# A Mamba block and a mixture of experts in one program: where a token tile's choice of experts stands, and which steps follow it

## The reference

```
xz = x @ W_in.T;  xs, z = halves of 512 channels
xc = silu(conv_4_taps(xs) + conv_b)            # causal, per channel
dt = xc @ W_x[:32].T
y  = xc * softplus(dt @ W_dt.T + b_dt) * silu(z)
x  = layernorm(2x + y @ W_out.T)

scores = sigmoid(x @ gate_w.T)                 # 16 experts in 4 groups
keep the 2 best groups (by their two best, with a bias), in them the 4 best experts
w = 2.5 * scores of the 4 / their sum
x = layernorm(2x + sum_k w_k * expert_k(x) + shared(x))   # each: (silu(x Wg) * (x Wu)) @ Wd
```

## Time and profile before

| | us |
|---|---|
| median of 3 runs | 664.12 |
| lowest, highest | 659.53, 667.1 |
| the profiled execution, its own time | 662.12 |
| its span in the profile | 660.4 |
| mean granted TensorE clock | 0.941 |
| PE busy | 544.3 (82%) |
| DVE busy | 416.6 (63%) |
| ACT busy | 376.1 (57%) |
| POOL busy | 322.4 (49%) |

### The profile page before, as it was taken

How to read it: one execution, slowest core, us unless ns; L and a number is a source line. 1 busy time by engine, 2 the same in 40 slices (tenths; PEclk the granted TensorE clock), 3 DMA queues, 4 the chain that set the end, 5 groups by cost and what they waited for, 6 DMA issues and landing times.

```text
span 660.4 us, 11746 instructions
## 1 busy us (share of the span) xinstructions
PE 544.3 (82%) x3143; PEld 459.7 (70%) x3143; DVE 416.6 (63%) x1123; ACT 376.1 (57%) x969; POOL 322.4 (49%) x361
## 2 busy tenths in 40 slices
PE   6897999999999999866686788788877778786884
PEld 5584767777676867555586687677877677776773
DVE  5795889888897988674442533333333365665686
ACT  4767677686858582813433544555554455556653
POOL 3502122675757576754654355554445555444510
PEclk9999999999999999997797788888898898899888
DMA  7973021323333223288354476444445676866578
GB/s 197 285 253 137 33 98 64 132 98 129 102 125 106 107 93 106 88 290 294 130 189 145 131 232 197 142 145 144 142 138 158 195 249 205 278 202 219 174 287 281
DMA packets 69094, 110.92 MB, mean 168 GB/s; under 512 B 11204, under 2 KB 52421, under 8 KB 68520
## 3 DMA queue, kind: packets, MB, share of 16 engines
q1 hardware_dynamic: 55800, 74.23, 36.2%
q0 software_dynamic: 12672, 35.67, 14.6%
q10 hardware_dynamic: 560, 0.27, 0.1%
HBM read 61.50 MB, written 49.69 MB: 168 GB/s over the span
## 4 chain that ended last, share of the span: by engine, by line
PE 32%; another core or an unknown queue 22%; ACT 19%; DVE 12%; issue 10%; DMA 2%; ACTq 2%; SPq 0%; POOL 0%; POOLq 0%; DVEq 0%
PE psum L824 4%; PE psum L758 4%; PE psum L760 4%; PE psum L759 4%; PE psum L902 3%; ACT y_out L1362 3%; DVE xc L1512 3%; ACT row L1362 2%; PE psum L1042 1%; ACT y_w L1373 1%; ACT y_pair L1362 1%; ACT y_ids L1371 1%; PE psum L793 1%; PE psum L1016 1%
## 5 line engine op out<-in xcount | busy, mean ns | idle before, releaser
L669 POOL DMA_INDIRECT x_buf<-row,row_id x128 | 127.6, 997 | 71.6 <-issue 45.9
L2122 DVE TENSOR_TENSOR e_act<-g_act,psum 128x512 f32<-128x512 f32 x36 | 24.6, 684 | 122.7 <-ACT g_act L1347 97.5
L1032 PE MATMUL psum<-ew_gu_hi,t_hi 128*128 x286 | 90.8, 318 | 1.8 <-issue 1.8
L661 POOL TENSOR_TENSOR m<-xc,zs 128x512 f32<-128x512 f32 x32 | 41.4, 1315 | 100.5 <-DVE shift L1590 57.4
L1034 PE MATMUL psum<-ew_gu_hi,t_lo 128*128 x286 | 87.3, 305 | 1.6 <-issue 1.6
L1033 PE MATMUL psum<-ew_gu_lo,t_hi 128*128 x286 | 87.3, 305 | 1.2 <-issue 1.2
L1347 ACT ACTIVATE g_act<-psum 128x512 f32<-128x512 f32 x36 | 21.6, 601 | 109.2 <-remote 100.1
L747 POOL DMA_INDIRECT y_buf<-y_out,y_ids x56 | 55.2, 985 | 58.1 <-ACT y_w L1373 22.1
L1512 DVE SCALAR_TENSOR_TENSOR xc<-psum,cw_taps,xc 128x511 f32<-128x511 f32 (+2 forms) x96 | 70.8, 739 | 5.3 <-ACT halo_x L1168 3.9
L1042 PE MATMUL psum<-ident,e_act 128*128 128x128 f32 x143 | 26.3, 312 | 53.0 <-DVE e_act L2122 44.3
L1032 PEld LDWEIGHTS psum<-ew_gu_hi,t_hi 128*128 128x128 f32 x286 | 61.8, 216 | 2.6 <-issue 2.6
(11 more groups left out here) (263 smaller groups left out, 1442.7 us busy)
## 6 DMA issues: line engine op xcount, KB each, us to landing
tiles_in<-x_buf SPq DMA_DIRECT2D x143, 144.0 KB
y_pair<-y_buf SPq DMA_DIRECT2D x20, 512.0 KB
y_in<-y_buf SPq DMA_DIRECT2D x12, 512.0 KB, 7.0
xT<-in_x_T SPq DMA_DIRECT2D x8, 512.0 KB
xtok<-in_x_tok SPq DMA_DIRECT2D x8, 512.0 KB
gu_hi_buf<-w_hi_now SPq DMA_DIRECT2D x8, 512.0 KB, 2.6
x_buf<-pad_row SPq DMA_DIRECT2D x17, 144.0 KB
raw_gu<-in_wg_T SPq DMA_DIRECT2D x16, 128.0 KB, 3.3
```

What stands on the lines that cost most here:

```text
L669: nc.gpsimd.indirect_dma_start(out=x_buf, out_offset=bass.IndirectOffsetOnAxis(ap=row_id[t % ROWS][:, b, k:k + 1], axis=0), in_=row[t % RO ...
L1032: pe.matmul(o, t_hi[par][:, k, r], w_hi, start=k == 0, stop=False)
```

## The change

On VectorE, five of the six steps of the choice leave the places between the root's steps and stand at the tile's end, among the subtractions `x1T_low`, `x_low` and `dt_low`. The steps of `place` for tile t-2 move up, from among the second chunk's convolution taps to among the first chunk's. On TensorE, `ranks` stands ahead of `dt_out`'s second half, the fourth block of `shared_down` moves from a tile's end behind the first half of the next tile's `dt_out`, and in tile 6 `dt_total` goes ahead of `gate`. On POOL, the row sends move up by about one block each, in the tiles and in the order behind them, and the results of the first five quads are sent one quad sooner. VectorE's and ScalarE's orders of tile 7 and of the expert stage are unchanged.

```diff
--- before.py
+++ after.py
@@ -677,7 +677,7 @@
 
             def quads_begun(q):
 
-                return min(q + (5 if q < 5 else 4 if q < NQ // 2 else 3), NQ)
+                return min(q + (4 if q < NQ // 2 else 3), NQ)
 
             pool.wait_ge(s["keep_one"], 2)
             pool.wait_ge(s["keep_ready"], N // seq_len)
@@ -696,38 +696,34 @@
             def tile(t):
                 at_least(pool, "y_done", PAIRS * t + 1)
                 gate_product(t, range(2, KI))
-                if t > 2:
-                    send(t - 3, range(3, SUB))
                 if t > 1:
                     send(t - 2, range(0, 1))
-                if t == NT - 2:
-                    return
+                    send_behind(t - 2, 1, "halo_added", PAIRS * (t + 1) + 1)
                 at_least(pool, "norm_ready", t + 1)
                 gate_product(t + 1, range(0, 2))
                 if t > 1:
-                    send(t - 2, range(1, 2))
+                    send(t - 2, range(2, 3))
+                if t == NT - 2:
+                    return
                 halo(t + 2)
                 if t > 1:
-                    send(t - 2, range(2, 3))
+                    send(t - 2, range(3, SUB))
 
             def last_tile(t):
-                send(t - 3, range(1, 2))
-                at_least(pool, "norm_ready", t)
-                gate_product(t, range(0, KI))
-                send(t - 3, range(2, 3))
-                send_behind(t - 3, 3, "res_done", 2 * (t - 2) + 1)
-                send_behind(t - 2, 0, "y_done", PAIRS * t + 1)
-                send_behind(t - 2, 1, "h_done", KS * (t - 1) + 1)
-                send_behind(t - 2, 2, "ln_in", 2 * (t + 1))
-                send_behind(t - 2, 3, "norm_ready", t + 1)
-                send_behind(t - 1, 0, "x1T_l", KD * (t + 1))
-                send_behind(t - 1, 1, "t_l", 2 * KD)
-                send_behind(t - 1, 2, "e_mul", 1)
-                send_behind(t - 1, 3, "a_l", 1)
-                send_behind(t, 0, "res_done", 2 * (t + 1))
-                send_behind(t, 1, "a_l", 2)
-                send_behind(t, 2, "a_l", 3)
-                send_behind(t, 3, "e_mul", 4)
+                gate_product(t, range(2, KI))
+                send(t - 3, range(3, SUB))
+                send_behind(t - 2, 0, "res_done", 2 * (t - 2) + 1)
+                send_behind(t - 2, 1, "y_done", PAIRS * t + 1)
+                send_behind(t - 2, 2, "h_done", KS * (t - 1) + 1)
+                send_behind(t - 2, 3, "ln_in", 2 * (t + 1))
+                send_behind(t - 1, 0, "norm_ready", t + 1)
+                send_behind(t - 1, 1, "x1T_l", KD * (t + 1))
+                send_behind(t - 1, 2, "t_l", 2 * KD)
+                send_behind(t - 1, 3, "e_mul", 1)
+                send_behind(t, 0, "a_l", 1)
+                send_behind(t, 1, "res_done", 2 * (t + 1))
+                send_behind(t, 2, "a_l", 2)
+                send_behind(t, 3, "a_l", 3)
             first_tile()
             for t in range(1, NT - 1):
                 tile(t)
@@ -936,13 +932,15 @@
             def tile(t):
                 x_proj(t + 1, 0)
                 dt_out(t, range(0, 2))
+                if t > 1:
+                    shared_down(t - 2, range(SUB - 1, SUB))
                 gate_turn(t - 1)
                 x_proj(t + 1, 1)
                 z_proj(t + 1, 0)
+                if t > 1:
+                    ranks(t - 2, t)
                 dt_out(t, range(2, KI))
                 shared_up(t - 1, 0)
-                if t > 1:
-                    ranks(t - 2, t)
                 x_proj(t + 1, 2)
                 out_proj_by_pairs(t)
                 z_proj(t + 1, 1)
@@ -953,12 +951,9 @@
                 shared_down(t - 1, range(0, 2))
                 transposes(t)
                 dt_in(t + 1)
-                if t < NT - 2:
-                    shared_down(t - 1, range(2, SUB))
-                    dt_total(t + 1)
+                shared_down(t - 1, range(2, SUB - 1))
+                dt_total(t + 1)
                 gate(t)
-                if t == NT - 2:
-                    dt_total(t + 1)
 
             def spin(n, bank=SPARE_BANK):
 
@@ -1088,7 +1083,6 @@
                     ranks(NT - 1, NT)
 
             t = NT - 1
-            shared_down(t - 2, range(2, 3))
             dt_out(t, range(0, 2))
             shared_down(t - 2, range(3, SUB))
             gate_turn(t - 1)
@@ -1977,28 +1971,30 @@
                 if not placed:
                     gate_logits(r)
                 softplus_product(t, 0)
-                conv(n, 0)
+                conv_tap(n, 0, 1)
+                if placed:
+                    place_rank(p)
+                conv_tap(n, 0, 2)
+                if placed:
+                    place_rows(p)
+                conv_tap(n, 0, 3)
+                if placed:
+                    place_top(p)
                 if t == TABLE_TILE:
                     first_ends()
                 softplus_sum(t, 1)
+                if placed:
+                    place_ids(p)
                 gate_one(r)
                 softplus_product(t, 1)
                 gate_score(r)
                 conv_tap(n, 1, 1)
-                if placed:
-                    place_rank(p)
                 gate_biased(r)
                 conv_tap(n, 1, 2)
-                if placed:
-                    place_rows(p)
                 group_pairs(r)
                 conv_tap(n, 1, 3)
-                if placed:
-                    place_top(p)
                 group_sums(r)
                 conv_halo(n, 0)
-                if placed:
-                    place_ids(p)
                 group_score(r)
                 if t < 2:
                     weights_low(PIECES_OF[t][0])
@@ -2019,17 +2015,12 @@
                 pick_top(r)
                 for b in range(SUB):
                     norm_mean(t, b)
+                norm_var(t)
+                root_bits(var[:, :], half_bits[:, :], "norm_step")
                 choose_compare(r)
-                norm_var(t)
-                choose_place(r)
-                root_bits(var[:, :], half_bits[:, :], "norm_step")
-                choose_above(r)
                 root_guess(rstd[:, :], half_bits[:, :], "norm_step")
-                choose_order(r)
                 root_z(var[:, :], **root)
-                choose_ties(r)
                 root_h(**root_of)
-                choose_sel(r)
                 root_once(**root_of)
                 root_h(**root_of)
                 root_series(root_z_[:, :], root_h_[:, :], "norm_step")
@@ -2044,14 +2035,19 @@
                 else:
                     for i in PIECES_OF[t]:
                         weights_low(i)
+                choose_place(r)
+                choose_above(r)
                 x1T_low(t)
+                choose_order(r)
                 if t < 2:
                     weights_low(PIECES_OF[t][2])
                 if more:
                     x_low(t + 2)
+                choose_ties(r)
                 if t == TABLE_TILE:
                     first_rows()
                 dt_low(n)
+                choose_sel(r)
                 if t < 2:
                     weights_low(PIECES_OF[t][3])
```

## The result

The changed kernel takes 665.99 us (median of 12 runs, 661.40 to 669.68) beside 664.39 (median of 12) for the kernel before in the same session: a ratio of 1.0102, interval 1.0062 to 1.0141. Those medians are only 0.24% apart, and the two profiled executions 0.65 us (662.77 and 662.12, spans 661.0 and 660.4). So the changed kernel is slower, by 1% in the ratio and by less in the medians, where 659 was forecast: inside the range, on the wrong side.

What follows compares the result with a forecast made beforehand. The prediction took the token tiles as bound by TensorE, with nearly all its idle time in one wait before the third dt product. 3.9 + 0.4 + 0.8 + 0.2 - 0.8 = 4.5 us off 662.12, plus 2.0 for the median: 659; range 650 to 668.

Steps and rivals of the forecast that it cites:

- TensorE's order: Token tiles: moving a shared_down block and ranks fills the wait before the third dt product, between 0 and 5.3 us.
- The term of 0.97 a tile: Steady token tiles: net gain of 0.97 us each from TensorE's new order, after a wait of 0.1 to 0.2 before out_proj.
- Tile 6: End of tile 6: the sooner root releases TensorE's shared_down, which waited 1.96 us, for a gain of 0.2.
- the 3.9: Tiles 3 to 6: 4 x 0.97 = 3.9 us gained by TensorE's new order.
- Tile 6 into 7: Gate of tile 6: its 0.76 wait is filled and dt_low comes sooner, gaining 0.8 us, between 0 and 0.9.
- slower rival: Hand-over: three long send runs each hold ScalarE one block longer, 9.9 us lost, to 674; chance 0.12.
- The picks: VectorE: moving picks to the tile's end nets nil there; the root ends about 0.2 us sooner.
- POOL holds nobody up: 0: Token tiles: POOL's reordered row sends and gate products delay no other engine, cost 0.
- The hand-over and the experts: Hand-over and expert stage: 2.8 us gained by one block fewer, 3.6 charged for longer runs, net loss 0.8.
- the mark of 5.3 us: Stretch 273 to 317: quad 0's g_act over 5.3 us later behind its x1T_lo means the slower rival is under way.
- The one block fewer in the experts' stage: Expert stage: one block of four sends fewer is left there, gain 2.8 us, at most 5.1.
- The terms for the tiles: Token tiles: 3.9 for tiles 3 to 6, 0.4 tile 2, 0.8 tile 6 into 7, 0.2 the sooner root.

Runs made afterwards that it cites:

- e9: e1 with POOL's whole program (sends, gate products, tail conditions, first results) as in the kernel before: 659.00 us, 0.9918 of the kernel before.
- e6: The changed kernel with e1's edit and, in tile 6, POOL's last gate product ahead of block 2's row sends: 658.49 us, 1.0026 of the kernel before.
- e7: The kernel before with only five of VectorE's picks moved to the tile's end, choose_compare standing twice: 656.16 us, 1.0005 of the kernel before.
- e10: e6 with the tail's row-send conditions and the first five quads' results as in the kernel before: 663.86 us, 0.9959 of the kernel before.
- e5: The changed kernel with POOL's second gate product of tiles 2 to 6 held until place_rows is over: 658.27 us, 1.0037 of the kernel before.
- e11: e4's kernel on another chip, where ScalarE is held: 670.13 us, 1.0153 of the kernel before.
- e4: The kernel before with only the changed tail conditions for row sends and first five results, on the 548.8 us chip: 548.77 us, 0.9996 of the kernel before.
- e8: The changed kernel itself, measured again in a second session: 659.86 us, 1.0106 of the kernel before.
- e2: The changed kernel with the old tail conditions for row sends and first five results, on the 548.8 us chip: 554.23 us, 1.0096 of the kernel before.
- e3: The changed kernel with the edits of e1 and e2 together, on the 548.8 us chip: 549.27 us, 1.0003 of the kernel before.
- e1: The changed kernel with place_rows, place_top and place_ids behind the second softplus sum, on the 548.8 us chip: 549.57 us, 1.0009 of the kernel before.

## Why the prediction was wrong

- **TensorE's order: the step that failed.** I wrote that the place steps, "some 0.5 us, which eats just the 0.5", now stand ahead of the second sum. I priced `place_rows` by its row in another place, with no POOL product beside it, and did not look what waits for the taps between which it was put. The term of 0.97 a tile measured 0: 1.09 gone before L808, 1.04 come before L754, because `place_rows` took 1.27 us beside POOL's product. Freed of the hold (e9) a tile gains 0.43: of the 1.09, 0.33 turns into a wait before `out_proj` (forecast 0.1 to 0.2), and the rest of the difference is gaps under 0.2 and matmuls that show 0.16 more busy time (33.57 in 34.07 us). So the term was also twice too large.
- **Tile 6, too small.** The forecast gave it 0.2 beside its share of the 3.9, for the wait of 1.96 before `shared_down`. That wait went whole, and tile 6 came 2.5 sooner although its own 0.97 did not come (1.9 sooner in e9).
- **Tile 6 into 7.** Forecast 0.8 sooner. `dt_low` comes 11.2 us behind `norm_ready` of tile 6 instead of 8.9, so 2.3 later, for the same reason, and the low clock behind the wait costs about 2.1 more. The prediction had asked of its slower rival whether long waits of TensorE bring the low clock, and priced nothing for it here. It hangs on POOL's order: I had costed the second pair of products behind four sends at 0, since its reader is late. Its reader is late; its neighbour on VectorE was not looked at. With that product ahead of the sends (e6) both costs are gone.
- **The picks.** Right: nothing (e7).
- **"POOL holds nobody up: 0".** Wrong twice over: the slot and table steps above, and the place of the sends. In tile 4 the run of eight ends 32.1 us behind `norm_ready` of tile 3 in e6, and 29.2 in e9, which has the old order of the sends; `sg` comes 1.5 us behind it in e6, and the period is 34.5 there (35.0 in e10) against 34.07. In e5, where the slot steps keep their early place, the period is 33.9 all the same.
- **The hand-over and the experts.** Forecast a net loss of 0.8, the first g_act at 320 to 325; it came at 332.0. The slower rival had the place and the sign right in part: the first g_act stood 8.69 us instead of 5.25 and the third 11.68 instead of 7.17, and the mark of 5.3 us was met (g_act of quad 0 came 5.7 later behind its x1T_lo); but the run of sixteen did not hold `sg` longer, and 5.3 of the 7.4 us were given back by the tenth quad. The one block fewer in the experts' stage, priced at 2.8, did not show: the row sends ended 6.2 us later than before. The tail alone costs 1.53% in the ratio (0.98 to 2.07) and 0.6% in the medians where the hold exists (e11), and nothing where it does not (e4).
- **The sum.** With the held steps and POOL's part undone (e9), the orders of TensorE and VectorE give 0.82%, 5.4 us (0.40 to 1.24%). The terms for the tiles summed to 5.3. That fit is luck in good part: in e9's trace the tiles give some 2.6 us up to `norm_ready` of tile 7, counted from that of tile 0, and the rest comes in the first quad.

How the losses share the 1% on chips with the hold, and how large the whole loss is there, is not settled. Undoing the slot steps' hold gives 0.7% between the ratios and 0.24% between the medians (e5 against e8), with intervals that overlap; the tail alone costs more than the whole change does. Where ScalarE is not held it is settled: e2 loses 5.4 us, and moving the slot steps (e3) gives 5.0 of them back. Nor is the cause of ScalarE's hold known: the same sends take the same 0.96 us with it and without it, and the records name no engine as the releaser.

## What to carry to other kernels

Before a small VectorE instruction with two SBUF inputs is moved, look at what POOL does at the new place: its cost is POOL's remaining time there, not its own, and it falls on whatever is queued behind it. Then ask who waits for the instructions between which it is put. Try a change of the order on one engine at a time: here the orders of TensorE and VectorE, with the slot steps placed later, won 0.8%, and POOL's lost it again. And look at TensorE's granted clock behind a new wait: here 2.1 us came on top of the 2.3 by which `dt_low` was late.

## What the runs showed that was not expected

- A 31-column VectorE step took 3.07 us instead of 0.19, a 64-column one 1.27 instead of 0.21 and, in e1, a one-column one 2.50 instead of 0.16, beside a POOL product with two SBUF inputs; a tap with a PSUM input was not slowed (0.75).
- The long table step began 0.5 us ahead of POOL's product by the records, while POOL was issuing a send (POOL's spans are rough); it ended with the product.
- Behind a wait of 2.7 to 3.2 us TensorE ran at the lower clock for some 7 us, and a 128x512 matmul took 0.63 us instead of 0.39; behind waits of 0.61 to 0.75 at the same place it did not.
- The same program takes 548.8 us on one chip and 658 to 666 on others. In e4 and e11, one program, the steady token tiles take the same 34.5 us; tile 7 differs by 14.5 us, and most of the rest lies in the experts' stage, where a quad takes 5.6 us with g_act released by TensorE on the one, and 8.0 us with g_act about 1 us behind POOL's fourth send on the others.
